# Loading the per-item words once per engine in a fused residual kernel, and keeping them in registers

## What is computed

```python
x = x + L0(x, W1, b1, v, kind)          # scores = tanh(x W1 + b1) v; softmax under one of 3 masks; pooled / count
x = x + L1(x, lang, W1[lang], ...)      # relu(x W1[lang] + b1) W2[lang] + b2; residual; layer norm, gamma, beta
x = x + L2(x, zX, zY, zR)               # 3-point differences over columns and over rows, plus zR * x * (1 - x)
x = x + L3(x, cat, W[cat], b[cat])      # x W[cat] + b[cat], W[cat] is 512 x 512, 64 categories
```

## Time and profile before

| | |
|---|---|
| median of 3 runs | 1097.93 us (1093.1 to 1098.07) |
| profiled execution | 1097.21 us, its span 1095.4 us |
| granted TensorE clock | 0.998 of full |
| PE busy | 1055.9 us, 96% of the span |
| DVE busy | 956.5 us, 87% |
| POOL busy | 710.9 us, 65% |
| ACT busy | 504.8 us, 46% |
| DMA | 268.92 MB, mean 246 GB/s |

### The profile page before, as it was taken

How to read it: one execution, slowest core, us unless ns; L and a number is a source line. 1 busy time by engine, 2 the same in 40 slices (tenths; PEclk the granted TensorE clock), 3 DMA queues, 4 the chain that set the end, 5 groups by cost and what they waited for, 6 DMA issues and landing times.

```text
span 1095.4 us, 23744 instructions
## 1 busy us (share of the span) xinstructions
PE 1055.9 (96%) x4912; PEld 656.8 (60%) x4912; DVE 956.5 (87%) x1962; ACT 504.8 (46%) x1422; POOL 710.9 (65%) x665
## 2 busy tenths in 40 slices
PE   6799999999999999999999999999999999999996
PEld 3565666656655656666665566665666565566562
DVE  5799989989989899999888888989898898999994
ACT  3444444444444444445444444444444444444441
POOL 3467667666666676667657666767665766667765
PEclk9999999999999999999999999999999999999999
DMA  8688798678779977876786868887879788897873
GB/s 346 199 260 236 247 293 244 203 250 254 245 230 288 298 239 237 246 229 203 228 266 193 265 198 255 269 266 235 269 241 262 228 268 237 288 276 226 244 241 115
DMA packets 134732, 268.92 MB, mean 246 GB/s; under 512 B 29139, under 2 KB 29157, under 8 KB 127173
## 3 DMA queue, kind: packets, MB, share of 16 engines
q1 hardware_dynamic: 97476, 199.83, 58.7%
q10 hardware_dynamic: 37120, 67.58, 20.4%
HBM read 243.21 MB, written 33.55 MB: 253 GB/s over the span
## 4 chain that ended last, share of the span: by engine, by line
PE 54%; issue 21%; POOL 17%; DVE 6%; DVEq 1%; ACTq 0%; ACT 0%; DMA 0%; POOLq 0%; SPq 0%
PE ps_out L429 23%; POOL b_wide L892 6%; PE ps_adapt L411 6%; PE bank_hidden L383 6%; PE ps_attn L361 6%; PE ps_pool L402 6%; POOL neighbours L873 4%; POOL react L879 3%; PE ps_x3T L419 3%; POOL rstd L865 2%; DVE x L764 2%; PE bank_scores L372 2%; PE bank_hidden L395 1%; DVE res L739 1%; POOL above L885 1%
## 5 line engine op out<-in xcount | busy, mean ns | idle before, releaser
L429 PE MATMUL ps_out<-w3s,x3T 128*128 x1024 | 490.1, 601 | 2.3 <-ACT x3T L496 2.3
L885 POOL TENSOR_TENSOR above<-above,below 128x512 f32<-128x512 f32 x128 | 166.7, 1303 | 226.7 <-DMA above<-x 223.7
L429 PEld LDWEIGHTS ps_out<-w3s,x3T 128*128 128x128 f32 x1024 | 185.1, 191 | 190.6 <-issue 188.7
L764 DVE SCALAR_TENSOR_TENSOR x<-above,wide_rows,react 128x512 f32<-128x512 f32 x128 | 189.5, 1481 | 13.9 <-POOL above L885 12.5
L879 POOL TENSOR_TENSOR react<-react,x 128x512 f32<-128x512 f32 x128 | 175.5, 1371 | 2.4 <-ACT react L539 2.4
L892 POOL TENSOR_TENSOR b_wide<-b_wide,x 128x512 f32<-128x512 f32 x128 | 173.1, 1352 | 1.7 <-DMA b_wide<-in_b 1.7
L865 POOL TENSOR_TENSOR rstd<-var_eps,minus_half 128x1 f32<-128x1 f32 x128 | 70.2, 549 | 132.0 <-DVE var_eps L731 131.9
L517 ACT ACTIVATE square_junk<-ps_adapt,neg_mean 128x512 f32<-128x512 f32 x128 | 88.1, 688 | 139.1 <-DVE neg_mean L692 139.1
L411 PE MATMUL ps_adapt<-w_all,hid 128*128 x256 | 133.0, 601 | 12.6 <-DVE x L746 12.2
L383 PEld LDWEIGHTS bank_hidden<-w_all,xts 128*128 128x128 f32 x1024 | 124.4, 192 | 28.4 <-issue 26.4
L383 PE MATMUL bank_hidden<-w_all,xts 128*128 x1024 | 137.2, 277 | 0.0
(11 more groups left out here) (111 smaller groups left out, 1281.3 us busy)
## 6 DMA issues: line engine op xcount, KB each, us to landing
w3s<-in_w SPq DMA_DIRECT2D x128, 1024.0 KB
xts<-in_xT ACTq DMA_DIRECT2D x128, 256.0 KB, 4.7
xs<-in_x ACTq DMA_DIRECT2D x128, 256.0 KB, 5.0
b_wide<-in_b SPq DMA_DIRECT2D x128, 256.0 KB, 4.2
out_x<-res SPq DMA_DIRECT2D x128, 256.0 KB, 3.4
below<-x SPq DMA_DIRECT2D x128, 252.0 KB
above<-x SPq DMA_DIRECT2D x128, 252.0 KB
below<-x SPq DMA_DIRECT2D x256, 2.0 KB
```

What stands on the lines that cost most here:

```text
L429: mm = pe.matmul(ps_out[j.ring(2)][:, :], x3T[:, j.ring(2), k * P:(k + 1) * P], w3s[:, bass.ds(wslot * (K * D) + k * D, D)], start=(k == 0 ...
L764: nc.vector.scalar_tensor_tensor(x3[:, q, :], above[:, q, :], zy_t[:, bass.ds(i.n, 1)], react[:, q, :], ALU.mult, ALU.add).then_inc(x3_rea ...
L885: nc.gpsimd.tensor_tensor(above[:, q, :], above[:, q, :], below[:, q, :], ALU.add).then_inc(rows_ready, 1)
```

## The change

The words of a table row are put in another order, FRESH, WSLOT, CAT, ITEM, LANG, KIND, and each engine keeps what it has loaded in Python names (`words`), that is in registers, until the item's last stage. SP loads four words at the head of the slot and none ahead of the store. PE loads LANG and KIND of s + 1 as one load of two words where it loaded LANG of s + 1, and still loads WSLOT of s - 4; the loads of KIND of s and LANG of s - 1 are gone. ACT loads ITEM and LANG of s + 1 as one load of two words, and its other two loads are gone. DVE and POOL only get an unused name. The order of all other instructions is kept.

```diff
-CAT, FRESH, WSLOT, ITEM, LANG, KIND, NPARAM = 0, 1, 2, 3, 4, 5, 6
+FRESH, WSLOT, CAT, ITEM, LANG, KIND, NPARAM = 0, 1, 2, 3, 4, 5, 6
...
             def slot(s):
                 if s.inside(B):
-                    cat, fresh, wslot = load_params(sp, CAT, 3, s)
+                    words[s.n] = load_params(sp, FRESH, 4, s)
+                    fresh, wslot, cat, _ = words[s.n]
                     shift_rows(s)
                     load_w3(s, cat, fresh, wslot)
                 if (s - 2).inside(B):
-                    item_m2, = load_params(sp, ITEM, 1, s - 2)
-                    store(s - 2, item_m2)
+                    store(s - 2, words[(s - 2).n][3])
...
-                if s.inside(B):
-                    kind, = load_params(pe, KIND, 1, s)
                 if j.inside(B):
                     wslot, = load_params(pe, WSLOT, 1, j)
-                if h.inside(B):
-                    lang_m1, = load_params(pe, LANG, 1, h)
-                if s.inside(B):
-                    attn_scores(s, kind)
+                if s.inside(B):
+                    attn_scores(s, words[s.n][1])
...
-                    adapter_up(h, lang_m1)
+                    adapter_up(h, words[h.n][0])
...
-                    lang_p1, = load_params(pe, LANG, 1, s + 1)
+                    words[(s + 1).n] = load_params(pe, LANG, 2, s + 1)
...
-                    item_p1, = load_params(act, ITEM, 1, s + 1)
-                    load_xT(s + 1, item_p1)
+                    words[(s + 1).n] = load_params(act, ITEM, 2, s + 1)
+                    load_xT(s + 1, words[(s + 1).n][0])
...
-                    item, = load_params(act, ITEM, 1, s)
-                    load_x(s, item)
+                    load_x(s, words[s.n][0])
...
-                    lang_m1, = load_params(act, LANG, 1, s - 1)
-                    relu(s - 1, lang_m1)
+                    relu(s - 1, words[(s - 1).n][1])
```

More of the change, by code:

```diff
@@ L281, in shift_rows @@
                     sp.dma_start(to[at:at + rows, q], x2[source:source + rows, q]).then_inc(shift_in[q], 16)
+            words = {}
             def slot(s):
                 if s.inside(B):
-                    cat, fresh, wslot = load_params(sp, CAT, 3, s)
+                    words[s.n] = load_params(sp, FRESH, 4, s)
+                    fresh, wslot, cat, _ = words[s.n]
                     shift_rows(s)
@@ L457, in slot @@
                     attn_project(s + 1)
-                    adapter_project(s + 1, lang_p1)
+                    adapter_project(s + 1, words[(s + 1).n][0])
                 elif (s + 1).inside(B):
-                    adapter_project(s + 1, lang_p1)
+                    adapter_project(s + 1, words[(s + 1).n][0])
                     attn_project(s + 1)
```

## The result

The changed kernel takes 1086.74 us in the median of 13 runs, the kernel before 1096.58 us in 13 runs beside them. The ratio is 0.9919, with a 95% interval of 0.9897 to 0.9942: **0.8% faster**. One of the 13 runs of the changed kernel (1100.03 us) fell in a slower state of the chip and is not in the ratio.

A forecast was written before the change was run, and what follows sets the result against it. It took PE's floor of 8.04 us a slot as the bound, with SP's queue as full. From 1097.9 us, -1 (SP) - 2 (PE) + 0.2 (prologue), about -3, gave 1095 us; range for 8 in 10: 1088 to 1102.

The forecast's parts named there:

- What bounds the kernel: PE's floor is 8.04 us a slot; SP's queue, 7.93 us, is as full; late row copies stall PE, 22.9 us lost.
- The removed load on SP: One-word load ahead of SP's store: its removal saves about 0.47 us a slot with the gap behind it.
- The fourth word: Longer load at SP's slot head: costs 0.26 us in ordinary slots, 0.4 with a matrix; net saving some 0.15 us.
- the second rival: Fourth word on SP nearly free: SP wins 0.35 us a slot, time 1089 us; chance 0.21.
- What it is worth: SP's saving counts only in 19 stalling slots, 5.7 us at best, against 31 slots with later copies; gain 1 us.
- On PE: Two loads between lines 402 and 372 go; ten slots where they outlast the matmuls lose 2.3 us; gain 2 us.
- On ACT and the prologue: ACT's relu up to 0.3 us sooner without gain; first xts transfer in the prologue loses 0.2 us once.
- The first (nothing): SP's gain swallowed at its own waits, PE's long loads come elsewhere; time 1098 us; chance 0.16 together with the fourth.
- the third (slower by the longer load): Four-word load directly ahead of SP's copies costs 0.8 us a word beside a matrix; time 1102 us; chance 0.13.
- The fourth: Registers don't hold and the words are read again; time 1098 us; chance 0.16 together with the first.
- What would show it: Profile signs: half the loads on PE, SP loads near 1.2 us, store wait some 35 us, adapter_up wait little under 12.

The follow-up runs named there:

- e5_store_load_back: Changed kernel with the one-word load of ITEM put back ahead of the store on SP; 1093.18 us, ratio 0.9987 to the kernel before.
- e4_pitch8_off1: Changed kernel with table rows 8 words apart, words starting at word 1, so no four-word load is 16-byte aligned; 1088.56 us, ratio 0.993 to the kernel before.
- e3_pitch8: Changed kernel with table rows 8 words apart, so every four-word load on SP is 16-byte aligned; 1087.72 us, ratio 0.9913 to the kernel before.
- e7_load_early: e3_pitch8 with SP's load for the next item moved between the issue of the matrix and the store; 1089.14 us, ratio 0.9946 to the kernel before.
- e6_one_more_load: Kernel before with CAT loaded once more on SP, one word, ahead of the bias transfer; 1097.67 us, ratio 1.0019 to the kernel before.
- q_before_small_w3: Kernel before with three quarters of each category matrix left out of its transfer from item 8 on; 1079.04 us, ratio 0.9842 to the kernel before.

## Why the prediction was wrong

**What bounds the kernel.** Right. PE's floor of 8.04 us a slot stands in all kernels, SP's queue was as full as PE, and the way from late copies over POOL and DVE to PE's wait at adapter_up carried the gain: the wait fell from 12.2 to 6.5 us, most of what was won.

**The removed load on SP.** Roughly right as a term: 0.47 us forecast; e5_store_load_back costs 0.44 us a slot.

**The fourth word: mis-sized, in sign too.** Where the load isn't aligned, e4_pitch8_off1 shows 0.24 in slots without a matrix (means of the head load 0.93 and 1.17 us), as forecast, but only 0.1 beside one (1.38 and 1.47), not 0.4: in these means the delay that the matrix brings falls on the load, not on each word. Where it is aligned to 16 bytes the load of four is 0.35 us shorter than that of three. In the mean of all slots the head load went from 1.12 to 0.99 us. So the net saving, forecast as 0.15 us a slot, measured 0.66. The words of the second rival, that the fourth word is nearly free, hold for half of the items, for a reason that it didn't have. The Trainium skill's floor of about 600 ns for a tensor_load ("DMA: Bandwidth & Descriptors", "Latency and other measured facts") is undercut here, by one-word loads of 0.28 us; its about 200 ns for each register ("Runtime: NRT & Kernel Launch", "Instruction fetch mechanics"), which the page gives for loads from HBM, fits the unaligned loads here too (on SP 1.06 us at least for four words, 0.44 for one, so 0.21 a word) and not the aligned ones.

**What it is worth: the step that failed.** The prediction said that SP gathers its lead over two or three slots only, that in 31 slots the removed load lay inside the wait at the store and the longer one would be added behind it, and took a gain of 1 us from SP. SP's part alone gives 0.996 and 0.994, 4 to 6 us. Three things were wrong in it. First, the size of the cut, as above: 0.15 us a slot for 0.66. Second, the removed load was not hidden in the wait: put back alone, it costs 0.44 us a slot and some 7 us of time (e5_store_load_back). Third, I priced the cut as if each slot stood alone. SP's own work was 7.93 us against a spacing of 8.2 us between slots, and with so little slack lateness is handed on from slot to slot; at 7.27 us the mean lateness of the copies is 0.29 us in place of 0.83, and copies over 1 us late are 7 in place of 47. How the miss divides among the three is open. At the price by word that the prediction reckoned with, the cut is 0.34 us and the gain 0.4 to 1.0% with PE's and ACT's parts (e4_pitch8_off1), more than forecast; with a cut of 0.22 us in another place it is at most 0.3% (e5_store_load_back), no more than forecast.

**On PE.** Confirmed in the trace: the ten slots lost there, 2.3 us, are gone, or nearly so, in every kernel with PE's part. In time it can't be told from nothing by itself (1.0011).

**On ACT and the prologue.** Nothing found. The one profile of the changed kernel reaches item 4 1.0 us later than that of before, but over all profiles this point lies between 57.5 and 64.0 us with no relation to the edits, so 0.2 us can't be seen there.

**Rivals.** The first (nothing) and the third (slower by the longer load) fell. The second named the right size and place, 1089 against 1086.7, with a chance of 0.21; its cause holds for every second item, and e4_pitch8_off1 shows that most of the gain can come without it. The fourth fell: SP has 122 loads in the window, PE 244.

**What would show it.** SP's wait at the store was to rise from 21 to some 35 us; it rose to 65.5. The loads were to be near 1.2 us; half are. The wait at adapter_up was to fall a little; it fell by 47%, just short of the half that I had named as the sign of a wrong size of the late copies.

**Open.** Whether the copies land late beside a matrix because they stand behind it in SP's own DMA queue or because all share the DMA engines: this wasn't tried. Why a load ahead of the store costs more than the same time at the head of the slot. Whether ACT's part is worth the last 0.1%. No version tried beats the changed kernel beyond the intervals.

## What to carry to other kernels

Look at the queue that issues DMAs as at an engine: sum its waits over a long stretch, and if they are a few per cent, a few tenths of a microsecond a slot can show in the time, until the slack is there; after that nothing more came here (e3_pitch8, e7_load_early). Don't expect the face value: here 0.66 us a slot, 80 us of queue time in all, gave 4 to 6. Price a cut in such a queue by what it does in the slots that stall, not in the average slot, and ask what else those slots have in common; here it was a matrix on its way, which the change doesn't touch. And four words that are loaded into registers at once should start at a multiple of 16 bytes; for two or three words the place made no difference here.

## What the runs showed of the hardware

- A register load of four words takes half the time when it starts at a multiple of 16 bytes: 0.61 against 1.19 us in the median (e3_pitch8, e4_pitch8_off1), 0.48 against 1.06 at least, and at least 0.305 us in e5_store_load_back, about what one word takes (0.28 to 0.30). Two words took 0.49 us on ACT. Three words took 0.96 us in the median on SP, aligned or not (kernel before).
- The price of a load depends on what its engine did ahead of it: the three-word load takes 0.96 us in the median with two DMA issues since the last load and 0.68 us with one (e6_one_more_load). One word takes 0.45 us on SP behind seven issues and 0.29 us behind one. Loads don't add up.
- A category matrix of 1 MB issued in the slot ahead makes an unaligned load longer, 1.47 against 1.17 us in the mean for four words (e4_pitch8_off1), with single ones up to 2.8 us. A load placed right behind the issue of the matrix isn't longer for it: 0.48 and 0.47 us (e7_load_early).
- The same matrix makes the row copies land later, by 1.1 us in the kernel before and 1.5 in e7_load_early, taken from POOL's start behind them. With a quarter of the matrix it is 0.3 us (q_before_small_w3).
